# One reduction for two PSUM banks, pairs of matmuls ahead of a step's other units, and attention results gathered by DMA

## The chip, the cores and the metric

The kernel runs on one core of a Trainium2 chip. The metric is the time of one execution on the device in microseconds (us); lower is better. The engines are TensorE (PE in the rows, its weight loads PEld), VectorE (DVE), ScalarE (ACT), GpSimd (POOL) and SyncE (SP), which issues all transfers here.

## The reference

Sixteen sequences of 512 tokens and 256 features go through two pre-norm layers. Layer 0 has a blockwise attention and a feed-forward with ternary weights, layer 1 a plain softmax attention and a tree of 8 x 255 nodes:

```python
x = x + _L0_attn_ref(_layernorm(x), w_q, w_k, w_v, w_o)
x = x + _L0_ffn_ref(_layernorm(x), fast_b, w_fc, w_proj, u, v, gate)
x = x + _L1_attn_ref(_layernorm(x), qkv_w, qkv_b, out_w, out_b)
x = x + _L1_ffn_ref(_layernorm(x), W_in, b_in, W_out)

# L0 attention, for each block of 256 keys, 16 heads of 16 features
s_blk = einsum('bhqd,bhkd->bhqk', q, k_blk) * scale
m = max(s_blk, axis=-1, keepdims=True)
e = exp(s_blk - m)
num = num + einsum('bhqk,bhkd->bhqd', e, v_blk)
den = den + sum(e, axis=-1, keepdims=True)
# at the end num / den, then @ w_o
```

The maximum is taken per block in layer 0 and per row in layer 1, and no rescaling between blocks takes place in layer 0, so the maxima have to be exact inputs of the exponentials.

## The kernel before, in words

Four sequences make a quad, and four quads run one after the other. A quad has eight attention phases (`i` from 0 to 7: the four sequences in layer 0, then the four in layer 1) and then a tree part of 32 iterations (`a`). Phase number over all is `n`. Phases 2 to 5 also carry a feed-forward (`ffn`); a phase prepares queries, keys and values of the next one (`prep`, not in phase 7) and finishes the attention of the one before (`post`, not in phase 0). "Light phases" are those without a feed-forward.

A phase has 16 steps `s`, one for each head. Every engine has its own list of instructions, written out by step, and semaphores join them. TensorE does in a step (L1170 to L1317):

- four pairs of matmuls. Each pair is one maximum tile (`maxima`, L1092 to L1099: the scores of head `s + 7`, queries on the partitions, into bank 0 or 1 by turns) and one score tile (`scores`, L1108 to L1115: head `s`, keys on the partitions, into banks 2 to 4). They use different halves of the rows of the array.
- after two pairs the weighted sum of the group of heads before (`weighted`, L1119 to L1129, bank 5), four column tiles side by side.
- other units, the "side units", in banks 6 and 7: one after the third pair and one after the fourth. They are the hidden layer and its output (`hidden`, `ffn_out`, L1165), queries, keys and values of the next phase (`qk_unit`, `v_unit`), transposes (`transposed`, `natural` L1135, `attn_T` L1140), the output projection (`projected`) and the transposed maxima (`maxima_rows`).

VectorE reduces each maximum tile as it comes (L824 by block in layer 0, L827 in layer 1), negated, and counts `max_rd` up; TensorE's next maximum tile waits on it for the bank. Seven heads ahead, these maxima are split into three fp16 parts by GpSimd, transposed by TensorE, copied by ScalarE (`row_read`) and sent by SyncE as six further rows of the query operand (`rows_up`, L345), so that the score matmul subtracts them. ScalarE takes the exponentials of two tiles (L617) or one (L614) at a time.

The attention result of a group of four heads lies in bank 5: 32 rows a head, of which 16 are values and one (row 16) is the sum of the exponentials, since the values have a column of ones. ScalarE copies it to `oT` (`out_read`, L596), the last group in step 3 of the next phase. There TensorE transposes it to tokens on partitions (`natural`, 4 transposes for each of four token tiles, steps 6 to 9), VectorE takes the reciprocal of 16 sums (L833) and multiplies (L835), TensorE transposes back (`attn_T`, steps 10 and 11), ScalarE and VectorE split into high and low fp16, and the projection follows in step 12. In the tree part the last phase's result goes the same way in iterations 2 to 4.

SyncE's list in a phase is: rows of group 1, the stacked queries or keys of the next phase (`stack_up`, six transfers each), rows of group 2, and so on. Queries and keys come out of ScalarE's `qk_read` (L575: high part, then an fp32 copy in a buffer of two), and GpSimd makes the low part.

## Time and profile before

| | |
|---|---|
| median of 3 runs | 3209.13 us (3197.66 to 3212.54) |
| profiled execution, whole time | 3217.72 us |
| its span, first to last instruction | 3215.9 us |
| granted TensorE clock, mean | 0.963 of full |
| busy: PE, DVE, ACT, POOL | 91%, 64%, 60%, 36% |
| chain that ended last, by engine | PE 71%, DVE 15%, ACT 5%, issue 4%, POOL 3% |
| maximum reductions (L824, L827) | 2048, 685 ns each |
| idle before the maximum's matmuls (L1099) | 185.5 us |

A row of the timeline gives start, duration, engine, line, operation, output<-input with shapes, a count of merged instructions and, in brackets, how long the engine was idle before and which instruction ended that. A mark x8 at a weighted sum stands for four matmuls, each recorded in two passes.

### The profile page before, as it was taken

The numbers are of one execution on the slowest core, as the hardware profiler recorded it, in microseconds if no ns is written. First come the engines' busy times: TensorE is split into PE (matmuls) and PEld (weight loads), VectorE is DVE, ScalarE is ACT, GpSimd is POOL, SyncE is SP. The second block draws the span as 40 slices with busy tenths as digits, with TensorE's granted clock in tenths as the row PEclk, the third lists the DMA queues.
The fourth block names the chain that finished last, engine by engine and source line by source line (L and its number), as shares of the span: only waits on it lengthen the run. The fifth ranks groups of instructions, "written<-read, shape, count | busy, mean of one in ns | idle before, by whom it ended". The sixth has DMA issues, their size and how long they took to land.

```text
span 3215.9 us, 50344 instructions
## 1 busy us (share of the span) xinstructions
PE 2934.8 (91%) x19007; PEld 1329.9 (41%) x19007; DVE 2073.3 (64%) x3769; ACT 1918.7 (60%) x2899; POOL 1151.0 (36%) x1535
## 2 busy tenths in 40 slices
PE   4789999899988999889998999989998899998999
PEld 1233333257523333326742333333763233332476
DVE  7676766744567777754467677675447766767544
ACT  3666666654466666664446666666445666666644
POOL 4234443135313444214431344421442144442244
PEclk7799999999989999999989999999998999999999
DMA  4100000000100000000010000000010000000000
GB/s 146 35 22 22 22 22 26 18 1 27 47 25 26 24 22 22 22 12 14 30 36 27 25 24 22 22 22 7 14 44 27 27 22 22 25 19 26 2 14 14
DMA packets 90432, 82.62 MB, mean 26 GB/s; under 512 B 15531, under 2 KB 89651, under 8 KB 90179
## 3 DMA queue, kind: packets, MB, share of 16 engines
q1 hardware_dynamic: 90191, 79.40, 7.4%
q8 instruction: 152, 2.49, 0.3%
q14 instruction: 89, 0.73, 0.1%
HBM read 17.48 MB, written 8.39 MB: 8 GB/s over the span
## 4 chain that ended last, share of the span: by engine, by line
PE 71%; DVE 15%; ACT 5%; issue 4%; POOL 3%; SPq 1%; DMA 1%; ACTq 0%; DVEq 0%; POOLq 0%
PE ps L1064 20%; PE ps L1099 12%; PE ps L1129 12%; PE ps L1343 10%; PE ps L1070 5%; DVE nmax L827 5%; DVE nmax L824 4%; PE ps L1165 4%; ACT arena L617 2%; PE ps L1115 2%; PE ps L1076 2%; PE ps L1334 2%; DVE stats L776 1%; DVE hT L810 1%; POOL h L434 1%
## 5 line engine op out<-in xcount | busy, mean ns | idle before, releaser
L617 ACT ACTIVATE arena<-ps 128x1024 f32<-128x1024 f32 x684 | 699.8, 1023 | 541.6 <-PE ps L1115 539.2
L1099 PE MATMUL ps<-kst,qst 48*128 48x512 f16 x2048 | 750.9, 402 | 185.5 <-DVE nmax L824 100.3
L824 DVE TENSOR_REDUCE nmax<-ps 128x2 f32<-128x512 f32 x1024 | 667.6, 685 | 325.2 <-PE ps L1099 320.6
L827 DVE TENSOR_REDUCE nmax<-ps 128x1 f32<-128x512 f32 x1024 | 668.2, 685 | 299.8 <-PE ps L1099 298.5
L1115 PE MATMUL ps<-qst,kst 54*128 54x512 f16 x2048 | 748.4, 400 | 36.1 <-ACT arena L617 31.3
L1129 PE MATMUL ps<-arena,vn 128*32 128x512 f32 x4096 | 566.6, 627 | 0.2
L1099 PEld LDWEIGHTS ps<-kst,qst 48*128 48x128 f16 x2048 | 165.0, 94 | 957.5 <-DVE nmax L824 350.6
L614 ACT ACTIVATE arena<-ps 128x512 f32<-128x512 f32 x680 | 405.6, 596 | 111.6 <-PE ps L1115 109.4
L530 POOL TENSOR_TENSOR arena<-arena 127x512 f16<-127x512 f32 (+1 forms) x256 | 290.7, 1156 | 425.6 <-ACT arena L769 425.6
L1343 PE MATMUL ps<-wout,arena 127*128 127x256 f16 (+1 forms) x3072 | 356.9, 272 | 0.0
L1064 PE MATMUL ps<-hT,win 128*127 128x512 f16 (+1 forms) x1536 | 353.2, 379 | 1.4 <-ACT arena L617 1.4
L769 ACT ACTIVATE arena<-arena 127x512 f16<-127x512 f32 (+1 forms) x256 | 161.2, 630 | 319.9 <-DVE arena L1042 316.3
L1042 DVE SCALAR_TENSOR_TENSOR arena<-ps,thr,arena 127x512 f32<-127x512 f32 (+1 forms) x256 | 180.1, 745 | 247.3 <-PE ps L1334 247.3
L1343 PEld LDWEIGHTS ps<-wout,arena 127*128 127x128 f16 (+1 forms) x3072 | 298.5, 98 | 58.0 <-issue 4.7
L439 POOL TENSOR_TENSOR parts<-qk,parts 128x512 f16<-128x512 f32 x128 | 151.8, 1187 | 420.5 <-ACT qk L583 420.5
L462 POOL TENSOR_TENSOR arena<-arena 128x512 f32<-128x512 f32 x128 | 133.2, 1041 | 317.6 <-ACT arena L625 315.3
L1064 PEld LDWEIGHTS ps<-hT,win 128*127 128x127 f16 (+1 forms) x1536 | 178.6, 117 | 156.6 <-ACT arena L617 5.0
L745 ACT ACTIVATE arena<-ps,bin_ 128x512 f32<-128x512 f32 (+1 forms) x256 | 161.8, 683 | 92.4 <-PE ps L1064 91.8
L1115 PEld LDWEIGHTS ps<-qst,kst 54*128 54x128 f16 x2048 | 168.0, 93 | 108.4 <-ACT arena L617 82.2
L445 POOL TENSOR_TENSOR npart<-nmax,zero 128x32 f16<-128x32 f32 x128 | 32.5, 254 | 498.3 <-DVE nmax L827 253.8
L1064 PE MATMUL ps<-hT,wfc 128*128 128x512 f16 x768 | 195.2, 392 | 0.0
L1129 PEld LDWEIGHTS ps<-arena,vn 128*32 128x32 f32 x4096 | 81.9, 109 | 162.2 <-issue 143.7
(118 smaller groups left out, 3278.7 us busy)
## 6 DMA issues: line engine op xcount, KB each, us to landing
qst<-parts SPq DMA_DIRECT2D x384, 64.0 KB, 2.6
kst<-parts SPq DMA_DIRECT2D x384, 64.0 KB, 2.6
x<-in_x SPq DMA_DIRECT2D x16, 512.0 KB, 4.0
out<-x SPq DMA_DIRECT2D x16, 512.0 KB, 2.9
qst<-nrow SPq DMA_DIRECT2D x256, 12.0 KB
arena<-in_winT SPq DMA_DIRECT2D x1, 2040.0 KB, 8.9
arena<-in_wfcT SPq DMA_DIRECT2D x1, 1024.0 KB, 7.9
arena<-in_wprT SPq DMA_DIRECT2D x1, 1024.0 KB, 9.8
```

Source lines behind the costliest of these rows:

```text
L530: nc.gpsimd.tensor_tensor(mlo[0:rows, a % 2, leaf, :], masked[0:rows, a % 2, leaf, :], mhi[0:rows, a % 2, leaf, :], ALU.subtract).then_inc ...
L614: nc.scalar.activation(pr[:, at, :], bank[4], ACT.Exp).then_inc(exp_rd, 1)
L617: nc.scalar.activation(pr[:, lo:hi + 1:hi - lo, :], ps[:, 2:4, :], ACT.Exp).then_inc(exp_rd, 1)
L745: nc.scalar.activation(actv[0:rows, a % 2, leaf, :], bank[2 + leaf][0:rows], ACT.Silu, scale=1.0 / WS, bias=bin_[0:rows, a % PAR, leaf:lea ...
L824: nc.vector.tensor_reduce(nmax[:, u, 2 * tt + half, :, slot], bank[tt % 2].rearrange("p (a s) -> p a s", s=BLK), AX.X, ALU.max, negate=Tru ...
L827: nc.vector.tensor_reduce(nmax[:, u, 2 * tt + half, 0, slot:slot + 1], bank[tt % 2], AX.X, ALU.max, negate=True).then_inc(max_rd, 1)
L1042: nc.vector.scalar_tensor_tensor(masked[0:rows, a % 2, leaf, :], sel_at(a, leaf)[0:rows], thr[0:rows, leaf:leaf + 1], actv[0:rows, a % 2, ...
L1064: ins = mm(out_ps, w[:, a, k, col:col + width], src[:, c, k, :], start=k + i == 0, stop=k == KD - 1 and i == 2)
L1099: mm(bank[tt % 2], qst[lo:hi, n % 2, e // 2, tt * P:(tt + 1) * P], kst[lo:hi, n % 2, e // 2, :], start=True, stop=True).then_inc(max_ps, 1)
L1115: ins = mm(bank[score_bank(i, tile)], kst[lo:hi, n % 2, s // 2, kt * P:(kt + 1) * P], qst[lo:hi, n % 2, s // 2, :], start=True, stop=True)
L1129: i = mm(bank[5][32 * j:32 * j + 32], vn[:, n % 2, at:at + 2 * HD], pr[:, HOME[n % PHASES * NG + g, j, kt][0], :], start=kt == 0, stop=kt ...
L1343: i = mm(bank[ACC[tt // 2]][:, tt % 2 * D:(tt % 2 + 1) * D], part[0:rows, a % 2, leaf, tt * P:(tt + 1) * P], wout[0:rows, w, c, leaf, :], ...
```

## The change

1. `maxima` on VectorE takes two tiles at once: one reduction reads banks 0 and 1 (1024 values) and counts `max_rd` up by two. TensorE's code for the tiles is unchanged; its waits on `max_rd` now pass only when the reduction over both banks is done.
2. On TensorE a step is pairs 0 and 1, the weighted sum, pairs 2 and 3, and then all side units of the step (`beside`), up to two of them together; they are laid out anew over the steps.
3. `natural` and `attn_T` go. `att_up` on SyncE copies the values of a head from `oT` to 16 partitions of `raw_att` (which is `h`'s memory), and the sums to a DRAM tensor with 16 copies of each row and back to `den`: per phase 2 transfers out, 8 between, 2 back. It stands between the rows of group 1 and the first stack. `divided` on VectorE takes the reciprocal of 512 sums and multiplies 512 values, twice, behind the second reduction of steps 6 and 7 (in iteration 3 of the tree part). The rows of `wo` are reordered on the host to match (`by_value`). Projections move to steps 10 and 11 (iteration 5).
4. The fp32 copy of queries and keys has one buffer and not two, so ScalarE's copy waits for GpSimd's low part of the one before. `oT` has four groups and not five. ScalarE's, VectorE's and GpSimd's lists are reordered to the new steps: statistics and moments of the next sequence end in step 1 where they ended in step 0, and the high and low parts of a feed-forward's input move from step 15 to step 0 of the next phase. SyncE sends the stacks 0 and 1 together before the rows of group 2.

The core of the diff (VectorE's step is shown with its new lines alone):

```diff
-        qk = sb("qk", [P, 2, S])
+        qk = sb("qk", [P, S])
...
+        oT = sb("oT", [P, NG, S])
+        den = sb("den", [P, KD, S])
...
+        raw_att = h[:].rearrange("p (k a) d -> p k (a d)", k=KD)
...
+        def sums(gh):
+            rows = oT[HD:P:2 * HD, 2 * gh:2 * gh + 2, :].rearrange("j k s -> j (k s)")
+            return bass.AP(rows.tensor, rows.offset, [rows.ap[0], [0, HD], rows.ap[1]])
...
+            def att_up(n):
+                for gh in range(2):
+                    sp.wait_ge(oT_sb, n * NG + 2 * gh + 2)
+                    if n:
+                        sp.wait_ge(att_in[gh], n * 80)
+                    sp.dma_start(spread[gh], sums(gh)).then_inc(den_out[gh], 16)
+                for gh in range(2):
+                    for j in range(G):
+                        rows = slice(gh * HALF + j * HD, gh * HALF + (j + 1) * HD)
+                        sp.dma_start(raw_att[rows], oT[32 * j:32 * j + HD, 2 * gh:2 * gh + 2, :]).then_inc(att_in[gh], 16)
+                for gh in range(2):
+                    sp.wait_ge(den_out[gh], n * 16 + 16)
+                    sp.dma_start(den[gh * HALF:(gh + 1) * HALF].rearrange("p k s -> p (k s)"),
+                                 spread[gh].rearrange("j r s -> (j r) s")).then_inc(att_in[gh], 16)
 
...
                     rows_up(n, 1)
                     if prep:
+                        sp.wait_ge(hT_ps, norm_at(b, norm_of(i + 1)) * KD + KD)
+                    else:
+                        sp.wait_ge(aT_lo, (n - 2) * KD + KD)
+                    if i:
+                        att_up(n - 1)
+                    if prep:
                         stack_up(n + 1, 0)
+                        stack_up(n + 1, 1)
                     rows_up(n, 2)
                     if prep:
-                        stack_up(n + 1, 1)
+                        stack_up(n + 1, 2)
                     rows_up(n, 3)
                     if prep:
-                        stack_up(n + 1, 2)
+                        stack_up(n + 1, 3)
                         rows_up(n + 1, 0)
-                        stack_up(n + 1, 3)
...
+                if n + c:
+                    act.wait_ge(qk_lo, n * 4 + c)
+                nc.scalar.activation(qk[:], bank[src], ACT.Identity, scale=scale, bias=bias).then_inc(qk_sb, 1)
...
+                if n:
+                    act.wait_ge(att_in[g // 2], n * 80)
+                nc.scalar.activation(oT[:, g, :], bank[5], ACT.Copy).then_inc(oT_sb, 1)
+
+            def attn_high(n, k, buf):
+                act.wait_ge(attn_sb, n * KD + (k + 1))
+                nc.scalar.activation(hT[buf][:, HI, k, :], raw_att[:, k, :], ACT.Copy).then_inc(aT_hi, 1)
...
+                    if s == 0 and ffn:
+                        hT_high(b, f"F{i - 2}", 0, 6)
+                        hT_high(b, f"F{i - 2}", 1, 7)
+                    if s == 1 and ffn:
+                        relu(f, 0)
+                    if s == 3 and prep:
+                        hT_high(b, nxt, 0, 6)
                     exps(b, i, s, 0)
...
+                    if s == 4:
+                        if prep:
+                            qk_read(n + 1, 0, 7)
+                        if ffn:
+                            relu(f, 3)
+                    if s == 5:
+                        if prep:
+                            qk_read(n + 1, 1, 6)
+                        if ffn:
+                            relu(f, 4)
...
+            def maxima(n, e, tt):
+                at = slice(2 * tt + half, 2 * tt + half + 3, 2)
+                dve.wait_ge(max_ps, n * (H * T) + (T * e + tt + 2))
+                if n // QUAD % 2 == 0:
+                    nc.vector.tensor_reduce(nmax[:, u, at, :, slot], ps[:, 0:2, :].rearrange("p t (a s) -> p t a s", s=BLK),
+                                            AX.X, ALU.max, negate=True).then_inc(max_rd, 2)
+                else:
+                    nc.vector.tensor_reduce(nmax[:, u, at, 0, slot], ps[:, 0:2, :], AX.X, ALU.max, negate=True).then_inc(max_rd, 2)
+
+            def divided(n, k):
+                for gh in range(2):
+                    dve.wait_ge(att_in[gh], n * 80 + 80)
+                nc.vector.reciprocal(den[:, k, :], den[:, k, :]).then_inc(rden_sb, 1)
+                dve.wait_ge(rden_sb, n * KD + (k + 1))
+                nc.vector.tensor_tensor(raw_att[:, k, :], raw_att[:, k, :], den[:, k, :], ALU.mult).then_inc(attn_sb, 1)
...
+                        maxima(*ahead, 0)
+                    if s == 0 and ffn:
+                        hT_low(b, f"F{i - 2}", 0, 6)
+                    if s == 0 and prep and not ffn:
+                        next_stats(0)
+                    if s == 1 and prep:
+                        if ffn:
+                            next_stats(1)
                         else:
+                            moments(b, nxt)
+                    if s == 3 and prep:
+                        hT_low(b, nxt, 0, 6)
+                    if s in (9, 10) and post:
+                        attn_low(n - 1, s - 9, POST_T)
                     if s == 12 and ffn:
                         ffn_scale(f, 0)
                     if s == 13 and after:
                         if after == "T0":
+                            after_attention(n - 3, 1)
                         else:
                             after_attention(n - 1, 1)
                         moments(b, after)
+                    if s == 14 and ffn:
+                        ffn_scale(f, 1)
+                    if s == 0 and ffn:
+                        hT_low(b, f"F{i - 2}", 1, 7)
+                    if s == 3 and prep:
+                        hT_low(b, nxt, 1, 7)
+                    if s == 12 and after:
+                        if after == "T0":
+                            after_attention(n - 3, 0)
+                        else:
+                            after_attention(n - 1, 0)
                     if ahead:
+                        maxima(*ahead, 2)
+                    if s == 0 and prep:
+                        next_stats(0 if ffn else 1)
+                    if s == 1 and ffn:
+                        moments(b, nxt)
+                    if s in (6, 7) and post:
+                        divided(n - 1, s - 6)
+                    if s == 7 and biased:
+                        values(n + 1, 0, 6)
+                    if s == 9 and biased:
+                        values(n + 1, 1, 7)
+                    if s in (11, 12) and post:
+                        attn_residual(n - 1, s - 11, 7)
...
+                if s == 0 and ffn:
+                    hidden(b, q, 0)
+                    hidden(b, q, 1)
+                if s == 1:
+                    if ffn:
+                        pe.wait_ge(relu_rd, f * M0 + 1)
+                        hidden(b, q, 2)
+                        pe.wait_ge(relu_rd, f * M0 + 2)
+                    maxima_rows(n, 1)
+                if s == 2 and prep:
+                    if ffn:
+                        pe.wait_ge(relu_rd, f * M0 + 3)
+                    elif i == 2 + QUAD:
+                        pe.wait_ge(scl_mul, (f - 1) * 2 + 2)
+                    transposed(b, nxt, 0, 6)
+                    pe.wait_ge(mrow_sb, n * NG + 2)
+                    transposed(b, nxt, 1, 7)
+                if s == 3:
+                    if ffn:
+                        pe.wait_ge(hT_lo, norm_at(b, nxt) * KD + 1)
+                        hidden(b, q, 3)
+                    if prep:
+                        hT_read(b, nxt, 0)
+                        hT_read(b, nxt, 1)
+                        qk_unit(n + 1, 0, PREP_T, 7)
+                if s == 4:
+                    if prep:
+                        if ffn:
+                            pe.wait_ge(relu_rd, f * M0 + 4)
+                        qk_unit(n + 1, 1, PREP_T, 6)
+                    if ffn:
+                        pe.wait_ge(qk_sb, (n + 1) * 4 + 1)
+                        hidden(b, q, 4)
...
+                if s == 6:
+                    if prep:
+                        if ffn:
+                            pe.wait_ge(relu_rd, f * M0 + 6)
+                        else:
+                            pe.wait_ge(qk_sb, (n + 1) * 4 + 2)
+                        v_unit(n + 1, 0, PREP_T, 6)
+                    if ffn:
+                        pe.wait_ge(mrow_sb, n * NG + 3)
+                        hidden(b, q, 6)
+                if s == 7:
+                    if ffn:
+                        pe.wait_ge(v_sb, (n + 1) * 2 + 1)
+                        hidden(b, q, 7)
+                    if prep:
+                        if ffn:
+                            pe.wait_ge(relu_rd, f * M0 + 7)
+                        else:
+                            pe.wait_ge(mrow_sb, n * NG + 3)
+                        qk_unit(n + 1, 2, PREP_T, 7)
+                if s == 8 and prep:
+                    if ffn:
+                        pe.wait_ge(relu_rd, f * M0 + M0)
+                    else:
+                        pe.wait_ge(v_sb, (n + 1) * 2 + 1)
+                    qk_unit(n + 1, 3, PREP_T, 6)
...
+                if s == 10:
+                    if ffn:
+                        pe.wait_ge(qk_sb, (n + 1) * 4 + 4)
+                        ffn_out(f, 0)
+                    if post:
+                        pe.wait_ge(mrow_sb, n * NG + 4)
+                        pe.wait_ge(aT_hi, (n - 1) * KD + KD)
+                        pe.wait_ge(aT_lo, (n - 1) * KD + KD)
+                        projected(n - 1, 0, POST_T, 7)
+                if s == 11:
+                    if ffn:
+                        ffn_out(f, 1)
+                    if post:
+                        pe.wait_ge(attn_upd, (n - 1) * 2 + 1)
+                        projected(n - 1, 1, POST_T, 7)
...
+                    for kt in (2, 3):
+                        if ahead:
+                            maxima(*ahead, kt)
+                        scores(b, i, s, kt)
+                    beside(b, i, s)
...
+def by_value(w):
+
+    return w.reshape(2, 2, D // 4, D).transpose(1, 0, 2, 3).reshape(D, D)
```

## Rows read from the trace of the kernel before

**Rows 1.** Windows: start:end length, busy (instructions) of PE to POOL, clock, DMA share, GB/s.

```profile
876.50:942.30 65.80, 53.12 (x294) 15.06 (x294) 43.88 (x78) 41.78 (x61) 11.63 (x25) 0.84 0.10 31
942.30:1007.70 65.40, 55.98 (x385) 19.70 (x385) 51.30 (x102) 44.81 (x68) 14.77 (x30) 1.00 0.09 30
1007.70:1088.00 80.30, 75.80 (x501) 30.09 (x505) 54.94 (x105) 53.08 (x84) 34.48 (x48) 0.98 0.07 22
1088.00:1166.00 78.00, 73.50 (x496) 29.70 (x494) 55.18 (x106) 51.85 (x81) 34.50 (x48) 1.00 0.07 23
1166.00:1244.50 78.50, 73.73 (x497) 29.75 (x497) 57.16 (x108) 52.80 (x82) 36.81 (x49) 1.00 0.07 22
1244.50:1322.90 78.40, 73.02 (x494) 29.12 (x496) 54.05 (x96) 51.91 (x80) 33.66 (x44) 1.00 0.07 22
1322.90:1392.20 69.30, 59.25 (x376) 19.80 (x374) 49.36 (x91) 42.87 (x62) 13.95 (x26) 0.93 0.07 25
1392.20:1444.40 52.20, 45.46 (x304) 14.16 (x302) 31.21 (x62) 38.62 (x55) 8.42 (x18) 1.00 0.01 3
1444.40:1659.30 214.90, 213.96 (x1413) 142.45 (x1413) 110.06 (x197) 94.63 (x152) 90.66 (x92) 1.00 0.08 26
1659.30:2446.60 787.30, 729.35 (x4745) 330.81 (x4745) 507.63 (x937) 472.65 (x720) 278.88 (x380) 0.97 0.07 23
```

**Rows 2.** Timeline of one light step, quad 0, phase 7.

```profile
626.33 0.39 PE L1099 MATMUL ps<-kst,qst 48*128 48x512 f16 x1
...
626.56 0.38 PE L1099 MATMUL ps<-kst,qst 48*128 48x512 f16 x1
...
626.75 2.48 DVE L827 TENSOR_REDUCE nmax<-ps 128x1 f32<-128x512 f32 x4 [0.60 <-PE ps L1099]
...
628.10 0.39 PE L1099 MATMUL ps<-kst,qst 48*128 48x512 f16 x1 [0.21 <-DVE nmax L827]
...
628.42 1.06 PE L1129 MATMUL ps<-arena,vn 128*32 128x512 f32 x8
...
629.41 0.09 PEld L1099 LDWEIGHTS ps<-kst,qst 48*128 48x128 f16 x1 [0.84 <-DVE nmax L827]
```

**Rows 3.** Timeline, a side unit in a feed-forward step.

```profile
384.28 1.47 PE L1064 MATMUL ps<-hT,wfc 128*128 128x512 f16 x6
...
385.68 0.39 PE L1099 MATMUL ps<-kst,qst 48*128 48x512 f16 x1
```

**Rows 4.** Groups by line: shapes, count | busy us, mean ns | idle before, releasers.

```profile
L1099 PE MATMUL ps<-kst,qst 48*128 48x512 f16 x2048 | 750.9, 402 | 185.5 <-DVE nmax L824 100.3 <-DVE nmax L827 64.5 <-DMA kst<-parts 6.8
```

**Rows 5.** One line's instructions: duration min/median/max in ns.

```profile
L932 DVE TENSOR_SCALAR oT<-ps x1: 1224/1224/1224, 24.2 to 24.2; 128x1024 f32<-128x1024 f32 x1
```

**Rows 6.** Groups by line again: reduction, transposes, copy, product, reciprocal.

```profile
L827 DVE TENSOR_REDUCE nmax<-ps 128x1 f32<-128x512 f32 x1024 | 668.2, 685 | 299.8 <-PE ps L1099 298.5
...
L1135 PE MATMUL ps<-idf,oT 128*128 128x128 f32 x512 | 81.8, 285 | 0.4
...
L580 ACT ACTIVATE parts<-ps 128x512 f16<-128x512 f32 x64 | 37.9, 593 | 53.3 <-PE ps L1064 53.1
...
L835 DVE TENSOR_TENSOR h<-ps,rden 128x256 f32<-128x256 f32 x128 | 54.3, 424 | 4.4
...
L833 DVE RECIPROCAL rden<-ps 128x16 f32<-128x16 f32 x128 | 31.7, 248 | 18.4 <-PE ps L1135 18.4
```

**Rows 7.** Timeline of SyncE's queue: six transfers of a stack.

```profile
374.72 3.79 SPq L342 DMA_DIRECT2D kst<-parts  x6
```

**Rows 8.** The page, DMA issues: KB each, median us from issue to landing.

```profile
kst<-parts SPq DMA_DIRECT2D x384, 64.0 KB, 2.6
```

**Rows 9.** Timeline of VectorE in one iteration of the tree part.

```profile
700.16 0.75 DVE L1005 TENSOR_SCALAR arena<-ps,binw 127x512 f16<-127x512 f32 x1
...
705.29 1.41 DVE L1042 SCALAR_TENSOR_TENSOR arena<-ps,thr,arena 127x512 f32<-127x512 f32 x2 [0.76 <-PE ps L1334]
```

## What the change should do to the time

> **What bounds the kernel now.** I read the page first (section 1: TensorE 91% busy, VectorE 64%, ScalarE 60%; section 4: 71% of the chain that ended last on TensorE), then cut one group of four sequences (a "quad") into its eight attention phases and its tree part, with the boundaries where the exponential of a phase's first tile begins [rows 1]. TensorE's busy column is a weak witness, since the ends are modelled; the useful thing in those rows is the length of each phase. Phases 2 to 5, which carry the feed-forward, take 78 to 80 us, 4.9 us for each of 16 steps. The phases without it take 65.8, 65.4, 69.3 and 52.2 us; the tree part takes 214.9.
>
> Next I looked inside one light step [rows 2]. The pair of tile 2 starts at 626.33, that of tile 3 at 626.56; VectorE's first reduction starts at 626.75, 0.42 us after its matmul, and four of them run back to back in 2.48 us (0.62 each). The weighted sum starts 0.32 us after the last pair (628.10 to 628.42), and the next pair 0.99 us after that (629.41). The step is 3.08 us: four reductions and 0.6 us in which VectorE waits. There are two banks, and a matmul fills one while VectorE reads the other. In a feed-forward step the side units fill the time: a unit of six 512-column matmuls runs from 384.28 to the next pair at 385.68, 1.40 us, and again 0.32 us pass from a pair to the unit [rows 3]. The waits of the weight loads for VectorE mislead: the last row of [rows 2] has 0.84 us of them under the weighted sum, whose stream TensorE has to finish anyway. The row of the maximum's matmuls has 185.5 us of idle time in front of them, 6% of the span [rows 4], and that is the most that a better order of these can return.
>
> **Edit 1, one reduction for two banks.** It reads 1024 values. No reduction of that form stands in the trace; the nearest is a one-input operation of VectorE on the same two-bank shape, 1224 ns [rows 5], and reductions of one bank take 685 ns, 0.62 when back to back [rows 2, 6]. Bounds: 1.10 us (twice 533 ns of streaming and little else) and 1.37 (twice 685); I take 1.22. For VectorE alone nothing is lost, 1.22 against 1.24. But the next pair of matmuls now needs both banks, so nothing overlaps any more: pair 0 at t, pair 1 at t+0.23, the reduction at t+0.65, its end at t+1.87, the next pair at t+1.94 (0.07 after a reduction's end, as in [rows 2]). A half step lasts at least 1.94 us, a step at least 3.88. Behind the first half lies the weighted sum, which needs 0.23+0.32+0.99 = 1.54; 0.4 us stay open in each. Behind the second half lie the side units: 0.55 us and 1.40 for one unit of six (1.95, just hidden), 3.2 for two.
>
> **Edit 2, pairs ahead of the side units.** A step with a unit in either gap loses one return to the pairs, 0.2 us (0.32 and the 0.1 after a unit, less what is streaming), in about 10 steps of a feed-forward phase: 2 us. It is in the sum below, since I add the units of a half without a gap between them.
>
> **Edit 3, results by transfers and a division of whole tiles.** Removed from TensorE in each phase: 24 fp32 transposes in six units, 0.43 of streaming and 0.1 of return for four of them, 3.0 us [rows 6]. Removed from VectorE: four reciprocals of 16 values (247 ns) and four products (424 ns), 2.7 us. Added to VectorE: two reciprocals and two products of 512 values. A product costs 0.69. The reciprocal is the unknown. A 16-value operation at one value a cycle would take about 152 ns and 17; the row has 247, so some 75 ns are extra. If they belong to the 16 values, one value costs about 6 ns and 512 cost 3.1 us; if they are a fixed cost, 512 cost 0.77. I take 3.1, as the plainer reading, and keep 0.77 and, for the end above, 4.4 (all but 115 ns going by value). The Trainium skill speaks against this edit: VectorE: DVE Perf Modes (First, the fixed hardware budget) says that the reciprocal is an iterative divide with a repeat count of 8. At 8 cycles a value 512 would need 4.3 us, and the whole would come out some 35 us above my sum; the row of 247 ns agrees with a slow divide but not surely with 8.
> One division (3.8 us) is queued behind the second reduction of steps 6 and 7, and the next reduction is queued behind it. Light phase: the two delay TensorE by 3.1 us each, 6.1. Feed-forward phase: side units hide half, 3.1 remain. In phases 3 to 6 VectorE also has the value copy of step 7, behind the second division, and TensorE waits for it ahead of two units: 7.1 instead of 3.1 (6.8 in phase 6).
> SyncE gets twelve more transfers per phase between two others, at 0.63 us an issue [rows 7] 7.6 us. The results' last group is copied in step 3, so issues end in step 5, and with 2.6 us from issue to landing, as for the 64 KB rows of the page [rows 8], the data are there at step 6, when VectorE asks. I cost this at nothing; if not covered it is 0 to 3 us a phase. The stack transfers and the rows of steps 8 queue behind them; the divisions delay TensorE more than these.
>
> **Edit 4, moved copies and moments.** With all pairs first, a unit meets the copy that frees its bank: ScalarE serves both exponentials (to about t+1.7), then two copies of 0.59 [rows 6], and only then the copy that the unit at t+2.5 wants. I count 1.1, 0.6 and 0.4 us in steps 4 to 6, 1.2 for residuals in steps 11 to 13, and, since the moments move from step 0 to step 1, GpSimd's normalisation ends too late for the transposes of step 2: 2.0 by hand, with what follows. 5.3 for a feed-forward phase, 1.7 to 3.9 for a light one.
>
> **The sum.** Feed-forward phase: 16 x 1.94 = 31.0 for the first halves; second halves 6 x 3.2 (steps 0, 3, 4, 6, 7, 8), 4 at the floor (7.8), 2 x 3.6 (steps 10, 11), 2.15, 2.15, 2.35, 2.6 for the rest, 43.4; with 5.3, 79.7; with divisions 82.8 (phase 2) and 86.8 (3 to 5). Against 80.3, 78, 78.5, 78.4 [rows 1]: +2.5, +8.8, +8.3, +8.4. Phase 0: 62.1 for 16 steps at the floor, 1.3 for the two units of step 8, 1.7 for copies, 3 for the low clock at its start (mean 0.84): 68.1, +2.3. Phase 1: 62.1+1.3+3.2+6.1 = 72.7, +7.3. Phase 6: 62.1+1.3+3.9+6.8 = 74.1, +4.8. Phase 7 has maxima in nine steps alone: 34.9+6.1+22 = 63, +11. Tree: 3.0 us of transposes go, and the divisions (7.6 us) lie in the 5.1 us between an iteration's decision and its products [rows 9] and in the 4 us by which the next selection is later: -3. Together +50 for the quad of the rows. The next quad takes 787.3 us where this one takes 782.8, for the same code [rows 1], so I take +46: four quads give +184. On the profiled execution's 3217.7 (its span and 1.8) that is 3402; it stands 0.27% above the median of the runs, so I forecast **3393 us**.
>
> **The rivals.**
> *A cheap reciprocal.* Divisions of 1.4 instead of 3.8 us take back 4.6, 2.6, 3 x 3.6, 5 and 4.6 us of a quad, 28: 110 in all, 3283. For it: nothing but that 75 ns may be fixed. Chance 0.20.
> *Faster after all.* The side units hide everything in the second halves, and the pairs ahead end today's waits. Then 165 us of waiting for VectorE go (100.3 and 64.5 of the 185.5 [rows 4]), 96 for transposes and 32 for switches, and 0.4 us in the first half of 484 steps come back, +194: 3119. Its point is the time from a first pair to the next free banks: it decides once second halves of light steps hold 1.4 us of other work. Against it: most of them hold one short unit or none. Chance 0.17.
> *The clock.* TensorE works some 1.8 of 3.88 us in an empty light step, against 1.8 of 3.08 now, and its granted clock is already 0.84 and 0.93 in phases 0 and 6 [rows 1]. With the lower level (1.2 GHz) in four tenths of the light phases, such a step costs about 1 us more, 23 a quad: 3485. Chance 0.12.
> *The transfers come late.* 3 us in each of 28 phases: 3477. This also covers the slower reciprocal. Chance 0.08. The Trainium skill (DMA: Bandwidth & Descriptors, Why a DMA increments its semaphore by 16 and not by 1) says that a transfer runs on the largest number of engines up to 16 that divides the outermost sizes of both sides; the transfer that repeats the denominators has 4 outermost, so it would run on 4 engines, which no transfer of the trace shows.
>
> **How the numbers follow.** The forecast has 0.43. Its own bounds (1.10 to 1.37 us for the reduction: about 60 us either way over 968 halves of which half are exposed) give 3330 to 3460. The range from 3200 to 3490 takes in the cheap reciprocal and the two upper cases and leaves the fast one out, with some of the rest 0.2. Below 0.5% is what a measurement of this kernel can hardly tell from no change. Faster 0.17, same 0.05, slower 0.78.
>
> **What would show it.** Right: reductions of about 1.22 us, each followed by some 0.7 us of idle VectorE with TensorE waiting; light steps of 3.9 us; a RECIPROCAL row of about 3 us with the longest waits of the maximum's matmuls in steps 6 to 8; phase 7 near 63 us and the tree part near 212. Wrong: a reciprocal under 1 us; reductions under 1 us; feed-forward phases under 76 us, which would say that the waits I added for copies are not there; VectorE waiting for the landing of the results.

## The result, and the profile after it

The changed kernel takes **3743.35 us** (3741.06 to 3753.35) against 3209.13 before: ratio 1.168, 95% interval 1.163 to 1.174. It is slower, as forecast, but by 534 us and not by 184; the time lies 253 us above the upper end of my range. The profiled execution has a span of 3739.3 us.

The page after, busy time and the groups that matter (columns as in [rows 4]: shapes, count | busy us, mean ns | idle before, releaser):

```profile
PE 2928.0 (78%) x18239; PEld 1226.5 (33%) x18239; DVE 2184.2 (58%) x2617; ACT 1922.2 (51%) x2899; POOL 1155.4 (31%) x1535
...
L1140 PE MATMUL ps<-kst,qst 48*128 48x512 f16 x2048 | 705.1, 429 | 535.8 <-DVE nmax L864 262.4
L867 DVE TENSOR_REDUCE nmax<-ps 128x2 f32<-128x1024 f32 x512 | 626.9, 1224 | 522.9 <-PE ps L1140 522.1
...
L872 DVE RECIPROCAL den<-den 128x512 f32<-128x512 f32 x64 | 214.1, 3345 | 50.0 <-DMA den<-spread 50.0
```

Every engine is busy for a smaller share than before: no engine became the bound, waiting did. The idle time before the maximum's matmuls is 535.8 us where [rows 4] had 185.5, and VectorE stands 1019.8 us before its reductions (522.9 and 496.9 in the two layers), nearly all of it until a matmul of TensorE ends: the two take turns. The reduction over two banks takes 1224 ns and the reciprocal of 512 values 3345; both were sized rightly.

Windows by phase for the same quad as in [rows 1] (start:end length, busy of PE to POOL, clock, DMA share, GB/s): phases 0 to 7, then the tree part.

```profile
1010.50:1081.90 71.40, 49.15 (x296) 12.93 (x296) 42.39 (x45) 41.89 (x62) 11.63 (x25) 0.83 0.10 30
1081.90:1169.60 87.70, 61.41 (x362) 17.08 (x360) 54.59 (x64) 45.11 (x67) 14.76 (x30) 0.82 0.17 38
1169.60:1255.40 85.80, 68.37 (x482) 26.05 (x480) 57.62 (x69) 52.56 (x84) 34.51 (x48) 1.00 0.17 39
1255.40:1350.30 94.90, 73.17 (x468) 26.45 (x464) 57.93 (x70) 52.03 (x81) 34.77 (x48) 0.89 0.14 35
1350.30:1444.70 94.40, 73.94 (x478) 27.52 (x480) 59.22 (x70) 52.97 (x82) 37.20 (x49) 0.89 0.15 35
1444.70:1538.20 93.50, 71.51 (x468) 26.10 (x472) 57.98 (x59) 51.50 (x80) 33.89 (x44) 0.91 0.15 36
1538.20:1624.40 86.20, 57.58 (x352) 16.32 (x349) 53.73 (x55) 43.32 (x63) 13.94 (x26) 0.84 0.16 39
1624.40:1697.50 73.10, 53.74 (x274) 11.75 (x276) 34.67 (x37) 37.89 (x53) 9.30 (x18) 0.72 0.11 23
1697.50:1925.20 227.70, 214.29 (x1397) 139.83 (x1395) 116.63 (x180) 95.92 (x154) 91.12 (x92) 0.98 0.11 31
```

All eight phases and the tree are longer, and the granted clock has fallen in seven phases. Now the inside of phase 1, steps 5 to 7 (timeline of PE, DVE and SP in part):

```profile
1100.41 10.75 SPq L361 DMA_DIRECT2D h<-oT  x8
...
1107.52 0.39 PE L1140 MATMUL ps<-kst,qst 48*128 48x512 f16 x1 [0.39 <-DVE nmax L864]
1107.74 0.38 PE L1140 MATMUL ps<-kst,qst 48*128 48x512 f16 x1
...
1108.23 1.22 DVE L864 TENSOR_REDUCE nmax<-ps 128x4 f32<-128x1024 f32 x1 [0.76 <-PE ps L1140]
...
1109.51 0.39 PE L1140 MATMUL ps<-kst,qst 48*128 48x512 f16 x1 [1.06 <-DVE nmax L864]
1109.73 0.38 PE L1140 MATMUL ps<-kst,qst 48*128 48x512 f16 x1
1110.22 1.23 DVE L864 TENSOR_REDUCE nmax<-ps 128x4 f32<-128x1024 f32 x1 [0.77 <-PE ps L1140]
...
1111.20 1.24 SPq L364 DMA_DIRECT2D den<-spread  x2
...
1116.45 3.35 DVE L872 RECIPROCAL den<-den 128x512 f32<-128x512 f32 x1 [3.01 <-DMA den<-spread]
1119.83 0.69 DVE L874 TENSOR_TENSOR h<-h,den 128x512 f32<-128x512 f32 x1
1120.44 1.22 DVE L864 TENSOR_REDUCE nmax<-ps 128x4 f32<-128x1024 f32 x1
...
1121.72 0.60 PE L1140 MATMUL ps<-kst,qst 48*128 48x512 f16 x1 [6.63 <-DVE nmax L864]
```

The handshake of edit 1 is plain: matmul at 1107.52, reduction at 1108.23, next pair at 1109.51. That is 0.71 + 1.22 + 0.06 = 1.99 us a half. Then the division: VectorE waits 3.01 us for the sums, divides for 4.0, reduces, and TensorE has stood for 6.63 us and restarts at the lower clock (a matmul of 512 columns takes 0.60 and not 0.39). VectorE waiting for the landing of the results was one of the signs of being wrong that the prediction named.

And step 7 of a feed-forward phase (4), TensorE and VectorE:

```profile
1388.90 0.39 PE L1140 MATMUL ps<-kst,qst 48*128 48x512 f16 x1 [1.83 <-DVE nmax L867]
...
1389.79 1.23 DVE L867 TENSOR_REDUCE nmax<-ps 128x2 f32<-128x1024 f32 x1 [0.95 <-PE ps L1140]
1390.94 3.34 DVE L872 RECIPROCAL den<-den 128x512 f32<-128x512 f32 x1
1394.31 0.69 DVE L874 TENSOR_TENSOR h<-h,den 128x512 f32<-128x512 f32 x1
1394.92 0.68 DVE L854 SCALAR_TENSOR_TENSOR vn<-ps,bv 128x512 f32<-128x512 f32 x1
...
1395.66 2.74 PE L1105 MATMUL ps<-hT,wfc 128*128 128x512 f16 x6 [5.97 <-DVE vn L854]
1398.20 2.08 PE L1105 MATMUL ps<-hT,wq 128*128 128x512 f16 x6
```

The unit that was to hide the division sits behind the value copy, which sits behind the division. TensorE waits 5.97 us, and the six matmuls that follow take 2.74 us where [rows 3] has 1.47.

### The profile page after: what moved, and what is told of

The parts are those of the page before. It is cut to its first block, busy times and chain, and to the rows that moved or that the text cites. A ratio compares the mean times of both kernels' runs of the same rounds, so it can differ in the third digit from the quotient of the medians.

```text
span 3739.3 us, 49288 instructions
## 1 busy us (share of the span) xinstructions
PE 2928.0 (78%) x18239; PEld 1226.5 (33%) x18239; DVE 2184.2 (58%) x2617; ACT 1922.2 (51%) x2899; POOL 1155.4 (31%) x1535
## 4 chain that ended last, share of the span: by engine, by line
PE 54%; DVE 24%; issue 8%; SPq 5%; ACT 4%; POOL 2%; DMA 2%; DVEq 0%; ACTq 0%; POOLq 0%
PE ps L1105 16%; PE ps L1140 14%; PE ps L1368 8%; DVE nmax L864 8%; DVE nmax L867 7%; DVE den L872 6%; PE ps L1170 5%; SPq L361 5%; PE ps L1111 4%; DMA den<-spread 2%; PE ps L1196 2%; PE ps L1117 2%; ACT arena L648 1%; PE ps L1156 1%; PE ps L1359 1%
## 5 line engine op out<-in xcount | busy, mean ns | idle before, releaser
L1140 PE MATMUL ps<-kst,qst 48*128 48x512 f16 x2048 | 705.1, 429 | 535.8 <-DVE nmax L864 262.4
L867 DVE TENSOR_REDUCE nmax<-ps 128x2 f32<-128x1024 f32 x512 | 626.9, 1224 | 522.9 <-PE ps L1140 522.1
L864 DVE TENSOR_REDUCE nmax<-ps 128x4 f32<-128x1024 f32 x512 | 626.3, 1223 | 496.9 <-PE ps L1140 495.5
L1156 PE MATMUL ps<-qst,kst 54*128 54x512 f16 x2048 | 713.7, 432 | 15.4 <-ACT arena L651 13.8
L1170 PE MATMUL ps<-arena,vn 128*32 128x512 f32 x4096 | 628.0, 690 | 0.0
L1140 PEld LDWEIGHTS ps<-kst,qst 48*128 48x128 f16 x2048 | 117.9, 96 | 1233.9 <-DVE nmax L864 525.9
L872 DVE RECIPROCAL den<-den 128x512 f32<-128x512 f32 x64 | 214.1, 3345 | 50.0 <-DMA den<-spread 50.0
L497 POOL TENSOR_TENSOR arena<-arena 128x512 f16<-128x512 f32 x128 | 147.9, 1156 | 83.2 <-ACT arena L663 83.2
```

Of the source, the lines that this page charges most:

```text
L864: nc.vector.tensor_reduce(nmax[:, u, at, :, slot], ps[:, 0:2, :].rearrange("p t (a s) -> p t a s", s=BLK), AX.X, ALU.max, negate=True).the ...
L867: nc.vector.tensor_reduce(nmax[:, u, at, 0, slot], ps[:, 0:2, :], AX.X, ALU.max, negate=True).then_inc(max_rd, 2)
L872: nc.vector.reciprocal(den[:, k, :], den[:, k, :]).then_inc(rden_sb, 1)
L1140: mm(bank[tt % 2], qst[lo:hi, n % 2, e // 2, tt * P:(tt + 1) * P], kst[lo:hi, n % 2, e // 2, :], start=True, stop=True).then_inc(max_ps, 1)
L1156: ins = mm(bank[score_bank(i, tile)], kst[lo:hi, n % 2, s // 2, kt * P:(kt + 1) * P], qst[lo:hi, n % 2, s // 2, :], start=True, stop=True)
L1170: i = mm(bank[5][32 * j:32 * j + 32], vn_at(n, at, 2 * HD), pr[:, HOME[n % PHASES * NG + g, j, kt][0], :], start=kt == 0, stop=kt == T - 1 ...
```

## The experiments

In each description "single" means one reduction for each bank. Times are medians, ratios are against the kernel before, measured beside it (medians 3206 to 3214). The kernel after has 1.163 to 1.174; where a run's interval overlaps that, the difference between the two medians is small against the noise, and the text says so.

**What are edit 1 and edit 3 worth?** Edit 1 undone in the kernel after:

```diff
-                dve.wait_ge(max_ps, n * (H * T) + (T * e + tt + 2))
-                    nc.vector.tensor_reduce(nmax[:, u, at, :, slot], ps[:, 0:2, :]..., negate=True).then_inc(max_rd, 2)
+                for tt in (tt, tt + 1):
+                    dve.wait_ge(max_ps, n * (H * T) + (T * e + tt + 1))
+                        nc.vector.tensor_reduce(nmax[:, u, 2 * tt + half, :, slot], bank[tt % 2]..., negate=True).then_inc(max_rd, 1)
```

> The changed kernel with edit 1 undone alone: VectorE reduces bank 0 and bank 1 one by one again, each counting by one; the order of the pairs, the transfers and the divisions stay. Theory A (the handshake of both banks opens gaps of 0.4 to 1 us in TensorE's stream in every half step, and these let its granted clock fall, from 242 us at the lower level before to 867 us after): the time falls from 3743 by 200 to 320 us, to 3420 to 3540, and the mean granted clock rises from 0.884 to 0.93 or more. Theory B (the divisions and the transfers before them make the loss, at steps 7 and 8): it falls by less than 100 us.

Measured: 3502.9, ratio 1.092 (1.090 to 1.095): edit 1 costs 240 us here, as theory A said, though the clock rose to 0.91 only and not to 0.93. The opposite, edit 1 alone put into the kernel before:

> The kernel before with edit 1 alone: one reduction for tiles 0 and 1 and one for tiles 2 and 3, the second at the place of the reduction of tile 3; nothing else changes, so the side unit between the third and fourth pair now lies inside the handshake. Theory A: 200 to 400 us slower than 3209, with a lower mean granted clock than 0.963. Theory B: less than 100 us slower.

Measured: 3599.6, 1.122 (1.119 to 1.124), clock 0.94. Alone, edit 1 costs 390 us, theory A. Next, the single version of the kernel after with all of edit 3 left out (`att_up`, `divided` and their waits go; results are neither gathered nor divided):

> The changed kernel with single-bank reductions and with all of edit 3 left out: no transfers of the results, no division, no transposes in their place; ScalarE takes whatever lies in the buffer, so attention's output is not computed. What is left is the new order (edits 2 and 4) minus the work of edit 3. If the new order is good in all phases as it is in phase 0, 3209 minus the 96 us of transposes minus 4 x 7 and more: 3050 or less. If the new order costs time in the feed-forward phases (88 to 92 us in e1_single against 78 to 80), more than 3150.

Measured: 3182.9, 0.991 (0.988 to 0.995), so the new order does cost time in the feed-forward phases. Edit 3 costs 320 us on top of this. The fourth corner, the same with the two-bank reductions:

> e9_nothird with the changed kernel's two-bank reductions: edit 1 in the new order with nothing of edit 3. The fourth cell of a table with e9 (3183), e1 (3503, edit 3 without edit 1) and the changed kernel (3743, both). If the costs add, 3183 and 240: 3423. If the stalls of edit 3 lower the cost of the handshake or the other way round, the difference from 3423 is their overlap; I expect 3420 to 3470, since the division behind the second reduction hides part of the handshake.

Measured: 3483.1, 1.085 (1.081 to 1.089). Edit 1 costs 300 without edit 3 and 240 with it; edit 3 costs 260 with two banks and 320 with one. The two overlap by 60 us; the overlap is larger than I expected (at most 47), with the sign that I expected. Together they make 560, 26 more than the loss of 534: what is left of edits 2 and 4, with the transposes gone and no result computed, stands 26 us under the kernel before.

**What in edit 3 costs?** The reciprocal replaced by a product with a constant (the division is left out), first in the kernel after, then in its single version:

```diff
-                nc.vector.reciprocal(den[:, k, :], den[:, k, :]).then_inc(rden_sb, 1)
+                nc.vector.tensor_scalar_mul(den[:, k, :], den[:, k, :], 1e-5).then_inc(rden_sb, 1)
```

> The changed kernel with each reciprocal of 512 values replaced by a multiplication by a constant, so it leaves the division out and its output is not the attention's. Every wait and transfer stays. The rows after show 64 reciprocals of 3345 ns, 214 us. Theory B: nearly all of it and the clock lost behind it come back, 200 to 260 us, to about 3510. Theory A: what side units hide does not come back, 120 to 180 us, to about 3590. If the late transfers and not the reciprocal set the wait at step 7, less than 100 us.

> The changed kernel with single-bank reductions (as e1_single) and with the reciprocals replaced by a multiplication by a constant (as e2_norecip: the division is left out, the output is not the attention's). If the two causes simply add: 3503 minus 148, 3355. Theory A, by which the handshake's gaps make the division cost more, expects less than that from the second step, 60 to 110 us: 3390 to 3440. If the division costs more once the handshake no longer hides it: 3300 or less.

Measured: 3595.4 (1.120, 1.116 to 1.125) and 3363.8 (1.048, 1.044 to 1.051): the reciprocal is worth 148 and 139 us, so this cost and edit 1's simply add. With the reciprocal gone and single reductions, 3364 is still 181 above 3183. Is that the transfers? The single version with its divisions but without the transfers (the reciprocals work on ones, nothing is gathered):

> e1_single without its transfers: reciprocals and products of 512 values stay in VectorE's steps 6 and 7 and in iteration 3, but work on ones and on what lies in the buffer, so no attention result is computed and nothing waits for a landing. Between e9 (3183, neither) and e1 (3503, both). Theory transfers late: about 150 of the 320 us are theirs, 3340 to 3370. Theory division: nearly all is, 3440 or more.

Measured: 3400.1, 1.060 (1.052 to 1.067). That lies between the two theories: the divisions alone cost 217 us over 3183, the transfers another 103; some 27 of these are in the tree (about 6.6 us a quad). Most of the rest is in step 7 of the phases 1, 6 and 7, which in the quad of the windows takes 13.6, 12.2 and 13.9 us with the transfers and 8.2, 6.7 and 6.9 without: VectorE waits there for the sums. Are the transfers late because of their order? The sums sent back before the second half of the values:

```diff
+                    if gh:
+                        back(0)
                     for j in range(G):
...
+                back(1)
```

> The changed kernel with the same transfers in another order: the four value transfers of groups 0 and 1 go out before SyncE waits for the last group, and the denominators of the first half come back before the second half's values. VectorE's wait for the denominators should end some 4 us earlier in each of 28 phases. Theory B: 60 to 110 us less, to about 3650. If the transfers are hidden, as the prediction had it, within 15 us of 3743.

> e5_single_norecip (single-bank reductions, the reciprocal left out) with the transfers in e3_order's order. e5 took 3364 us and e9, without any of edit 3, 3183; step 7 of the light phases took 11 to 12 us in e5 and 3.5 to 5 in e9. Theory transfers late (VectorE waits at step 6 for denominators that land too late): the 4 us by which they come sooner come back in each of 28 phases and in the tree parts, 80 to 120 us, to 3245 to 3285. Theory length of the instructions (the two products and copies on VectorE make the difference): within 20 us of 3364.

Measured: 3730.5 (1.163, 1.159 to 1.166), 13 us less than the kernel after, and 3340.4 (1.041, 1.037 to 1.045), 23 less than its own base. VectorE's wait for the sums fell from 50.0 to 21.6 us in the first and from 96.4 to 58.2 in the second. The first stays within the 15 us that "hidden" allowed, and its interval overlaps that of the kernel after; the second misses both of its theories, the nearer one by 4 us. An earlier landing gives back less than the wait that it removes. The other way to meet a late transfer, the divisions a step later:

```diff
-                    if s in (6, 7) and post:
-                        divided(n - 1, s - 6)
+                    if s in (7, 8) and post:
+                        divided(n - 1, s - 7)
```

> The kernel after with the two divisions of a phase one step later, at steps 7 and 8 instead of 6 and 7; nothing else is changed. VectorE waits 50 us in 18 places for the sums that the transfers spread, part of it in the steps and part in the tree, where the place of the division is not changed. Theory one, that the transfers land too late for step 6 and VectorE's standing still is a cost of its own: the waits in the steps go and the time falls by 15 to 60 us, 3685 to 3730. Theory two, that it is the division's 3.3 us itself wherever it stands, the waits in the steps being hidden or small: 3735 to 3755.

Measured: 3765.1, 1.173 (1.169 to 1.177), 22 us slower (the intervals overlap), which neither theory said. The wait did go, as the same row of the waits (waited for: us, times, longest) of the kernel after and of this one shows:

```profile
DVE den L872 <- DMA den<-spread: 50.0, 18, 6.5
```

```profile
DVE den L872 <- DMA den<-spread: 26.6, 5, 7.2
```

What is left are the tree's waits of some 6.5 us. But another wait has taken its place, in TensorE's rows of the later division:

```profile
PE ps L1140 <- DMA qst<-nrow: 45.5, 8, 6.2
```

These are the rows of the maxima of group 2 (`rows_up`), which step 8 needs. They are issued behind the twelve transfers of `att_up` and the twelve of the two stacks. In phases 1 and 6 of every quad TensorE stands 5.3 to 6.2 us for their landing in this run; in the kernel after no matmul waits for them, because TensorE has by then lost its time in step 7 to the division. The new transfers delay two things, and taking away the first wait uncovers the second. That the transfers cost nothing in the kernel after does not follow from this run. In phases 3 to 5 step 9 also grew, from 5.0 to 5.5 us to 7.2 to 8.0; I read this as the high and low parts of the result, which the projection of step 10 wants, coming late in turn. That reading was not tested.

**Is the order of the pairs what matters?** Pairs ahead of the side units, alone in the kernel before:

```diff
+                    if ahead:
+                        maxima(*ahead, 3)
+                    scores(b, i, s, 3)
                     ...side unit...
-                    if ahead:
-                        maxima(*ahead, 3)
-                    scores(b, i, s, 3)
```

> The kernel before with one edit: the fourth pair of maxima and scores of a step (tile 3) is issued ahead of the step's side units instead of behind them. Everything else, the single-bank reductions, the copies by engines, the queues of VectorE, GpSimd and ScalarE, is as before. The prediction took 2 us for each of the 16 phases with feed-forward units from this (edit 2), which is -32 us: 3177, ratio 0.990. Rival one, that the order is neutral because the exponentials of tile 3 that come sooner are waited for by nobody: 3209, ratio 1.00. Rival two, that the order costs, since the maxima of the next step are finished before the side units and the reductions of VectorE then stand unused while the side unit runs, and the last pair has no cover left: +1 us a step with a side unit in 128 steps, 3340, ratio 1.04.

Measured: 3207.7, 0.999 (0.997 to 1.001): neutral, the first rival. The same with the two-bank reductions:

> The kernel before with the two-bank reductions (3600 by themselves) and with the fourth pair ahead of the side units. Two banks need both banks free before the next two maxima products start; with the side unit behind the fourth pair it covers the last reduction of a step, with the side unit between the third and the fourth pair it covered the wait between them. Theory one, a side unit covers one of the two waits of a step wherever it stands: 3580 to 3610, no difference. Theory two, the old place left the fourth pair waiting for a reduction that began only once the fourth product, behind the side unit, was done, so that the side unit stood inside the handshake and hid nothing: about 0.6 us in each of 180 steps with a unit and as much again by the clock, 3420 to 3500. The kernel with everything but the third edit measured 3483, so theory two says that the order of the pairs makes nearly all of the 117 us between 3600 and 3483.

Measured: 3487.5, 1.086 (1.084 to 1.089), 112 us less than two banks without it, theory two. The edit that gives nothing with one bank is worth 112 us with two. The cause stands in the timeline of the kernel with two banks alone, where a unit of transposes lies between the third and the fourth maximum:

```profile
1245.55 0.39 PE L1102 MATMUL ps<-kst,qst 48*128 48x512 f16 x1 [0.39 <-DVE nmax L828]
...
1245.87 0.66 PE L1079 MATMUL ps<-idf,h 128*128 128x128 f32 x4
...
1246.45 0.39 PE L1102 MATMUL ps<-kst,qst 48*128 48x512 f16 x1
...
1246.95 1.23 DVE L828 TENSOR_REDUCE nmax<-ps 128x4 f32<-128x1024 f32 x1 [1.46 <-PE ps L1102]
...
1248.23 0.39 PE L1102 MATMUL ps<-kst,qst 48*128 48x512 f16 x1 [0.80 <-DVE nmax L828]
```

The reduction needs both matmuls. With the unit between them VectorE is idle for 1.46 us, where it is 0.76 with the pairs together (phase 1 above), and TensorE then waits 0.80 for VectorE.

**What do the moved copies and moments cost?** Between 3487.5 and 3483.1 lie the relaid units and copies of edit 4, and 96 us of transposes less: 4 us in all. With single reductions it is 25 us, 3207.7 and 3182.9. If the transposes are worth their 96 us, the rest costs some 92 and some 71 us. The rows of the transposed maxima (`maxima_rows`) show where; first the kernel before, then the one with two banks and without the third edit:

```profile
L1105 PE MATMUL ps<-idb,npart 128*24 128x128 f16 x512 | 52.9, 229 | 3.7 <-POOL npart L451 3.7
```

```profile
L1108 PE MATMUL ps<-idb,npart 128*24 128x128 f16 x512 | 56.2, 239 | 66.7 <-DVE vn L828 34.5 <-POOL npart L458 32.2
```

There are 63 us of new waits in front of one group: half for the value copy on VectorE, half for GpSimd. Another 24 us of waits for the value copy lie before feed-forward units; all waits for it were 8.7 us before. GpSimd's half in the single version, phase 1, step 13:

```profile
979.23 1.02 POOL L435 TENSOR_TENSOR rstd<-vpe,mhalf 128x4 f32<-128x4 f32 x1 [17.40 <-DVE vpe L819]
980.22 0.24 POOL L452 TENSOR_TENSOR npart<-nmax,zero 128x32 f16<-128x32 f32 x1
...
981.58 0.58 PE L1109 MATMUL ps<-idb,npart 128*24 128x128 f16 x4 [3.54 <-POOL npart L458]
```

GpSimd stands 17.4 us for VectorE's moments while the split of the next phase's maxima, which could run, is queued behind. The entry put back in front:

```diff
+                if prep:
+                    split_maxima(n + 1, 0)
                 if 1 <= i <= QUAD:
                     rstd_of(b, f"F{i - 1}")
...
-                if prep:
-                    split_maxima(n + 1, 0)
```

> The kernel after with single-bank reductions and without the third edit (3183), with one thing more: on GpSimd the split of the next phase's first maxima stands ahead of the reciprocal standard deviation again, where the kernel before has it. The third edit's absence and the place of all other copies and moments are unchanged. In the trace of the run without this, TensorE's product that spreads the maxima waited 35.9 us in 20 places for GpSimd's split, which stood behind a wait of 17 us for VectorE's moments. Theory one, that queue position is a cost of the moved moments: -36 us of the wait and some 20 us more by the clock that fell behind it, 3125 to 3150. Theory two, the wait moves to the next thing in TensorE's queue, which needs the normalised rows that come later by as much: 3175 to 3190.

> The kernel after with one entry of GpSimd's queue moved: the split of the next phase's first maxima stands ahead of the reciprocal standard deviation, as in the kernel before; nothing else is changed and nothing is left out. In the kernel with single-bank reductions and without the third edit this gave -33 us (3183 to 3150). Theory one, the wait is a part of the 534 us that adds to the others: TensorE's product that spreads the maxima waits 30.9 us in 16 places for it in the kernel after, so 3743 - 30 = 3713 and down to 3690 with the clock. Theory two, the two-bank reductions and the divisions set the pace and swallow it: 3735 to 3750.

Measured: 3149.9 (0.981, 0.979 to 0.984), -33 us, where nothing is gathered or divided; and 3721.8 (1.160, 1.156 to 1.164), -22 us in the kernel after itself. In the first theory one holds, at the upper end of its range. The second lies between its two theories (up to 3713, from 3735), nearer to the first, and its interval just touches that of the kernel after; TensorE's wait for the split went from 30.9 us to 0.4.

**What does the clock cost?** Short matmuls that nobody reads, behind the weighted sum and behind the units in steps 0 to 8 of phase 7. The first run has eighteen more at the start of steps 7 and 8; the second, shown here, has fourteen in these steps behind the weighted sum:

```diff
+                    if not prep and s < 9:
+                        keep_going(14 if s in (7, 8) else 1, bank[6])
...
+                    if not prep and s < 9:
+                        keep_going(5, bank[6])
```

> The changed kernel; in the phases numbered 7 alone TensorE gets dummy matmuls into the idle bank 6: 18 at the start of steps 7 and 8, and in steps 0 to 8 one behind the weighted sum and five behind the fourth pair. They depend on nothing and nobody reads them. In the changed kernel phase 7 takes 73 us, 43 of them at the lower clock. Theory clock (the low level itself costs, by slower pairs inside the handshake): with under 10 us low the phase falls to 60 to 66 us, the kernel by 28 to 52. Theory gaps alone (the handshake's time is VectorE's, and the clock rides along): phase 7 stays at 71 to 76 us even with the clock up.

> As e6_fill7, with the many dummies (14) moved from the start of steps 7 and 8, where they held up a pair that did not wait, to behind the weighted sum, where TensorE waits for the division. Phase 7 took 73.3 us on average in the changed kernel with 43 us at the lower clock, 71.3 in e6 with 10. Theory clock: 64 to 68 us. Theory gaps alone: 70 to 73 us.

Measured: 3744.6 (ratio 1.166, 1.163 to 1.170) and 3729.4 (1.162, 1.158 to 1.167); both intervals overlap that of the kernel after, so the phases say more than the totals. The second, phase 7 of the quad shown:

```profile
1625.80:1694.40 68.60, 61.05 (x354) 17.30 (x356) 36.24 (x37) 37.77 (x53) 8.83 (x18) 0.95 0.12 25
```

The clock is 0.95 and not 0.72, and the mean of the four phases 7 fell from 73.3 to 69.4 us, between the two theories; in the first run it was 71.3, which speaks for the gaps. The share of time at the lower level (1.2 of 2.4 GHz) is 2 x (1 - clock), so some 34 us less of it gave back 3.9. But this is a balance and not the clock's price, because the fill takes TensorE's time too: steps 7 and 8, with the fourteen, took 10.50 and 7.01 us where the kernel after has 7.99 and 5.85. A price without a fill stands in two traces, for step 1 of phase 7 in the same quad: the kernel after, at the lower level throughout, and the one with two banks and without the third edit, at the full one.

```profile
1629.05:1634.30 5.25, 4.40 (x21) 0.79 (x22) 2.45 (x2) 2.11 (x3) 0.90 (x4) 0.50 0.01 3
```

```profile
1520.57:1524.54 3.97, 2.53 (x22) 0.60 (x22) 2.45 (x2) 2.11 (x3) 0.91 (x4) 1.00 0.02 4
```

The same work takes 1.28 us more: 0.24 us for each at the lower level. The whole run has 867 us at the lower level (clock 0.884), the one before 240 (0.963). As an estimate, 630 x 0.24 = 150 us of the 534 are the clock's. The price is that of a light step; where TensorE does not wait it is higher, as the six matmuls of 2.74 and 1.47 us above show.

**A version that beats both.** The new order in phase 0 alone, on the kernel before, then with the pairs ahead in the other light phases too:

> The kernel before, with the changed kernel's order of units, copies and transfers in phase 0 of each quad alone, with single-bank reductions; phase 0 has no result to gather, so edit 3 has no part in it. In e1_single this phase took 59.4 us against 66.0 before. If the new order is what shortens it, the kernel falls by 20 to 30 us, to about 3183 (0.8% faster). If the shorter phase only hands its time on to phase 1, no change within 0.5%.

> The kernel before with the new order of phase 0 (which gave 3181 by itself, ratio 0.990) and with the pairs ahead of the side units in the phases without feed-forward units alone. If the order of the pairs gives something only where the steps are light in side units, this is below 3181 by 0.5 us for each of the 12 phases other than phase 0, 3175, ratio 0.988 or less. If the order is neutral, ratio 0.990 again. If the order costs wherever a side unit no longer stands inside the handshake of the maxima, 3190 to 3220.

Measured: 3181.3, 0.990 (0.988 to 0.992), phase 0 59 us instead of 66; and **3174.9, 0.989** (0.987 to 0.991). That is 34 us under the kernel before. Both intervals lie below 1, and they overlap each other; the gain of the first is phase 0's, and what the second adds is not clear of the noise. Which part of the new order shortens phase 0 was not tested.

## Why the prediction was wrong

The sign and the handshake as a mechanism held, the sum did not. Forecast and measured for the quad of the windows, in microseconds (the last pair of columns without the divisions, against the kernel with two banks and without the third edit):

| | before | forecast | after | forecast, no edit 3 | measured, no edit 3 |
|---|---|---|---|---|---|
| phase 0 | 65.8 | 68.1 | 71.4 | 68.1 | 71.9 |
| phase 1 | 65.4 | 72.7 | 87.7 | 66.6 | 76.7 |
| phase 2 | 80.3 | 82.8 | 85.8 | 79.7 | 86.1 |
| phases 3 to 5 | 234.9 | 260.4 | 282.8 | 239.1 | 261.9 |
| phase 6 | 69.3 | 74.1 | 86.2 | 67.3 | 73.7 |
| phase 7 | 52.2 | 63.0 | 73.1 | 56.9 | 65.3 |
| tree | 214.9 | 212 | 227.7 | 212 | 217.2 |
| sum | 782.8 | 833 | 914.7 | 790 | 852.8 |

Of the 82 us a quad that I missed, 63 lie in edits 1, 2 and 4 and 19 in edit 3. The four quads make 328 of the 350 us between 3393 and 3743.

**The step that failed is the net price of edit 1.** Take edit 1 out of the column without edit 3: the quad of 782.8 loses 8 for edit 2 and 24 for the transposes and gains the 30 that I had for copies, 781. I had thus put edit 1 at 9 us a quad, 36 in all. The two runs without edit 3 differ by 300 (3483.1 and 3182.9). The rest of that column was not too cheap: edits 2 and 4 without edit 3 came out 26 us under the kernel before, where my sum has 8.

- **Edit 1, the reduction and the handshake: right, 3% short.** 1224 ns against 1.22. A half lasts 1.99 us and not 1.94: from a pair to the reduction it is 0.71 and not 0.65. Over 968 halves 0.05 us are 48 us at most.
- **Edit 1, the cover and the clock: wrong.** I let the side units hide second halves, left 0.4 us open in first ones, counted the light phases as sixteen steps at the floor and gave the clock 3 us in phase 0 alone. Without edit 3 seven of the sixteen steps of phase 1 stayed at 4.0 us; the others took 4.7 to 6.4. Two estimates from the traces say what the 300 are made of. In the run with single reductions and without edit 3, 220 steps with maxima are shorter than 3.98 us, the light step with two banks at the full clock; lengthening each to 3.98 adds 147 us. And the run with two banks has 592 us at the lower level against 279, at 0.24 some 75. The other 80 or so I can't place. I also never asked what two banks cost without edit 2: the runs say 390 alone and 278 with the pairs ahead. My sum for a feed-forward phase with edits 1 and 2 alone (74.4 without the 5.3 for copies, and 3.0 more for the transposes that stay) was 77.4; that kernel has 82.7.
- **Edit 2: wrong for one bank** (-1.3 us measured, -32 forecast, so the 2 us a phase were not there), and blind to its real use, making edit 1 bearable.
- **Edit 4: about right in the sum, wrong in the places.** I counted waits for ScalarE's copies, 120 us in all, but of the queue positions only the moments in step 1. The split behind `rstd_of` (32 us of waiting, 22 to 33 when put right) and the value copy that `maxima_rows` and the feed-forward units wait for (58 us, 8.7 before; no run put it right) have no term in the sum. I had named the value copy only as what stands behind a division. In all, the new places and copies cost some 71 to 92 us, less than my 120, so this did not make the miss.
- **Edit 3, the reciprocal: right.** 3345 ns against 3.1 us, 148 us in all; my rival of the cheap reciprocal priced the difference between 3.1 and 0.77 at 110. The repeat count of 8 (the Trainium skill, VectorE: DVE Perf Modes, First, the fixed hardware budget), read as 8 cycles a value, gives an estimate of 4.3 us or 8.3 ns a value; the row has about 6.5 ns a value, and the measurement decides. In feed-forward phases 3 to 5 the division costs 7.0 us (282.8 against 261.9, by three), as forecast 7.1.
- **Edit 3, the transfers: wrong at nothing.** Ten transfers took 12.0 us to issue in phase 1 (1100.41 to 1112.44), where I had 7.6 for twelve. The row of `h<-oT`'s issues (minimum, median, maximum in ns) says why:

```profile
L361 SPq DMA_DIRECT2D h<-oT x256: 531/595/2264, 190.1 to 3551.1; - x128
```

  The median is the 0.6 us that I took, but single issues take up to 2.26 us. In all 32 groups of eight the second and the third take 1.9 to 2.3 us each, and the first up to 2.2. These stand right behind the transfer that spreads the sums. Whether that transfer runs on 4 engines, as the rule of the Trainium skill (DMA: Bandwidth & Descriptors, Why a DMA increments its semaphore by 16 and not by 1) cited in the prediction would have it, no run here told apart. The way back lands after 4.0 us and not 2.6. In the single version transfers cost 103 us. Phases 1 and 6 grew by 11.0 and 12.5 with edit 3 where I had 6.1 and 6.8, and the tree by 10.5 where I had nothing: the iteration's decision is queued behind a division that waits 6.49 us for the sums. The rows of the maxima behind these transfers come late as well, hidden as I had written by the divisions, and only by them.
- **The rivals.** The clock did fall, about as far as that rival said (some 0.80 over the light phases), and its price of 1 us a step was near, a little low: a light step takes 5.25 us at the lower level and 3.97 at the full one. The clock fell in the feed-forward phases too (0.89 to 0.91 in phases 3 to 5), which the rival left out, and so it is worth some 150 us and not 92. "Transfers late" held as a mechanism, yet moving the divisions away from the wait uncovered the next one. The rivals were priced one at a time on top of the forecast; they came together, and that alone puts the time out of a range that held each of them. The "faster" rival's 3119 starts from the profiled execution's 3217.7; from the median it would have been 3110.
- **What is not settled.** Of the 252 us in edits 1, 2 and 4, at most 48 are the longer half, some 80 the two new waits, and some 85 the clock (592 against 240 us at the lower level, by 0.24). These are estimates and can overlap, since the clock also falls behind the waits. The 40 or so that are left I can't place; they may be in side units that hide less of a reduction than I let them, but no run shows it by itself. No run held the clock up over the whole kernel.

## What to carry over

Two buffers that one engine fills while another reads are worth more than one saved instruction: an operation that takes both at once saved 16 ns here (1224 against twice 620) and cost 240 to 390 us. Before a reduction or copy is merged, work out the turn from the first fill to the next free buffer, and put nothing of other work between the fills of one merged operation. When units are moved, go down every engine's list and ask of each entry that waits what stands behind it and could have run; and when a transfer replaces engine work, look for a row of a transfer of that very shape and place, for its issue too, and ask what is issued behind it. A wait that can be removed without gain may only have covered another: look in the new trace for what the engine waits for now. And a fill that is meant to hold the clock takes time of its own, so compare like steps at both levels before its balance is called a price.

## What the runs showed of the hardware that I had not expected

- An issue is not of one length. Eight `h<-oT` of 64 KB took 10.75 us in phase 1, and in all 32 groups the second and third take 1.9 to 2.3 us each, where a `kst<-parts` of 64 KB takes 0.63 as a rule [rows 7]. Why the long ones stand behind the transfer with 16 copies of each row was not tried.
- A reciprocal over 512 values per partition takes 3345 ns, the product of the same shape 690.
- The granted clock falls to the lower level behind stalls of a few microseconds (6.63 and 5.97 us in the timelines above), and the six matmuls behind the stall took 2.74 us instead of 1.47. Yet a light step, in which TensorE waits for VectorE, takes 5.25 us at the lower level and 3.97 at the full one: 0.24 us for each microsecond at the lower level. The six matmuls that nothing held up lost 0.46 (1.27 us of 2.74).
